# Keys and values of all eight batches formed at the head of each attention and kept; in the second attention GpSimd adds the mixture's sum to x, and VectorE's order is changed

## The reference

```python
x = x + L0_xcond(layernorm(x), ctx, ctx, tau, delta, ...)   # attention to 64 context rows, 16 heads of 16
x = x + L0_ffn(layernorm(x), ...)     # 8 experts, top 2; then layernorm(out + input) * ln_g + ln_b
x = x + L1_xcond(...)                 # the second attention
x = x + L1_ffn(...)
x = x + L2_xcond(...)                 # another kind of attention, with a window
x = x + L2_ffn(...)                   # 8 experts, top 2
x = x + L3_xcond(...)                 # the third attention
x = x + L3_ffn(...)

def xcond(q, k, v, tau, delta, ...):  # x is (8, 512, 256), k = v = ctx is (8, 64, 256)
    qh, kh, vh = q @ Wq.T + bq, k @ Wk.T + bk, v @ Wv.T + bv
    a = softmax((qh . kh * tau + delta) / 4)
    return (a . vh) @ Wo.T + bo
```

## Time and profile before

| | |
|---|---|
| median of 3 runs | 2288.46 us (2286.05 to 2291.26) |
| the profiled execution | 2285.1 us, its span 2283.3 us |
| busy | PE 86%, PEld 64%, DVE 57%, ACT 41%, POOL 26% |
| first attention | 8 us to about 215 us |
| second attention | 631 us to about 870 us |
| third attention | 1888 us to about 2100 us |

### The profile page before, as it was taken

The page is one execution under the profiler, slowest core; times in us unless marked ns, Lnnn a source line. Parts: engine busy times, 40 slices in busy tenths (PEclk is TensorE's granted clock), DMA queues, the critical chain, the costliest instruction groups (busy, mean ns, idle before and its releaser), DMA issues. The chain is left out here.

```text
span 2283.3 us, 37863 instructions
## 1 busy us (share of the span) xinstructions
PE 1963.4 (86%) x11930; PEld 1465.4 (64%) x11931; DVE 1310.2 (57%) x2973; ACT 941.4 (41%) x2050; POOL 593.6 (26%) x582
## 2 busy tenths in 40 slices
PE   6998569999848887999989739999999995998687
PEld 3665536666525553666666729999999983665355
DVE  5885456666558887787655162222222215887987
ACT  3444324444336543333222413333333323553787
POOL 1122246666424431011000032222222221321000
PEclk9999579999959998999989559999999997999899
DMA  7001211111141104000000611111111114100001
GB/s 268 1 1 56 77 49 63 61 64 60 53 162 56 56 1 162 0 1 0 0 15 5 240 33 33 37 34 37 34 37 37 37 31 157 40 20 1 10 28 38
DMA packets 71122, 119.54 MB, mean 52 GB/s; under 512 B 13648, under 2 KB 54736, under 8 KB 67952
## 3 DMA queue, kind: packets, MB, share of 16 engines
q1 hardware_dynamic: 55760, 78.76, 9.9%
q0 software_dynamic: 13680, 37.37, 5.2%
q10 hardware_dynamic: 1584, 2.13, 0.3%
HBM read 86.90 MB, written 31.33 MB: 52 GB/s over the span
## 5 line engine op out<-in xcount | busy, mean ns | idle before, releaser
L1421 ACT ACTIVATE e_hT<-psum,x_bt 128x128 f32<-128x128 f32 x568 | 154.6, 383 | 336.4 <-PE psum L1384 331.7
L1384 PEld LDWEIGHTS psum<-e_xT,e_w 128*128 128x128 f32 x2272 | 268.3, 194 | 8.4 <-ACT e_xT L1414 4.9
L268 POOL TENSOR_TENSOR rstd<-lnt,half 128x4 f32<-128x4 f32 (+1 forms) x72 | 73.3, 1018 | 769.6 <-DVE lnt L262 769.6
L1384 PE MATMUL psum<-e_xT,e_w 128*128 128x128 f32 x2272 | 268.9, 277 | 4.2 <-ACT e_xT L1414 4.2
L1393 PE MATMUL psum<-m_w,e_hT 128*128 x1136 | 256.8, 379 | 0.0
L1393 PEld LDWEIGHTS psum<-m_w,e_hT 128*128 128x128 f32 x1136 | 210.4, 190 | 25.7
L1442 DVE COPY e_w<-m_w 128x2048 f32 x71 | 87.1, 1227 | 234.4 <-PE psum L1384 230.0
L724 DVE TENSOR_REDUCE a_mx<-psum 128x8 f32<-128x512 f32 x192 | 123.2, 684 | 84.0 <-PE psum L515 83.4
L1241 ACT ACTIVATE e_hT<-psum,x_bt,x_gt 128x128 f32<-128x128 f32 x284 | 106.9, 457 | 142.1 <-PE psum L1208 142.1
L1325 POOL DMA_INDIRECT rows_out<-e_y,dst x106 | 106.0, 1000 | 205.7 <-DVE e_y L1452 175.0
L1317 POOL DMA_INDIRECT e_x<-rows_in,src x142 | 142.3, 1002 | 56.8 <-issue 35.2
(11 more groups left out here) (282 smaller groups left out, 3588.2 us busy)
## 6 DMA issues: line engine op xcount, KB each, us to landing
m_w<-in_L_ffn_w SPq DMA_DIRECT2D x16, 1024.0 KB, 9.3
m_w<-in_L_ffn_w SPq DMA_DIRECT2D x16, 512.0 KB, 12.7
rows_in<-r_work SPq DMA_DIRECT2D x16, 512.0 KB, 5.4
m_w<-rows_out SPq DMA_DIRECT2D x16, 512.0 KB, 5.9
a_ar_g<-rows_out SPq DMA_DIRECT2D x16, 512.0 KB, 5.0
x_res<-in_x SPq DMA_DIRECT2D x8, 512.0 KB, 7.1
m_w<-rows_in SPq DMA_DIRECT2D x8, 512.0 KB, 3.9
out_x<-x_res SPq DMA_DIRECT2D x8, 512.0 KB, 3.0
```

What stands on the lines that cost most here:

```text
L1384: mm = pe.matmul(h_b[s][:, f, :], w1[:, kk, f * P:(f + 1) * P], xT[s][:, kk, :], start=(kk == 0), stop=(kk == DC - 1))
L1421: g = act.activation(hT[s][:, f, :], h_b[s][:, f, :], ACT.Gelu, bias=bt[:, bass.ds(e * FC + f, 1)])
```

## The change

All three attentions: the tile `kv` (8 batches x 256 columns) holds keys and values without bias. PE forms them for batches 0 to 3 ahead of `turn(0)`, into the banks that scores and transposes use later, and those of batches 4 to 7 right behind them in the second and third attention, behind the first scores in the first. ACT copies two batches at a time to `kv`, ahead of everything else that it does (in the first attention the last two copies stand behind the queries). DVE's `drain_keys` and `drain_values` read `kv` and not PSUM, and `drain_keys(b + 1)` stands at t == 1 in place of `drain_keys(b + 2)` at t == 3. PE's `keys_values` at t == 3 is gone. SP issues the eight context loads ahead of x (first attention) or between the first and the second fetch (the others). Second attention: `add_sum(b + 2)` goes from DVE's t == 2 to GpSimd, behind `gain(b + 2)` and ahead of `sum(b + 3)`.

```diff
@@ sync
+                if coming:
+                    coming.fetch(sp, 0)
                 for b in range(NB):
-                    if loading and b:
+                    sp.dma_start(cx[:, b, :, :], a["ctxT"][b]).then_inc(cx_in[b], 16)
+                if coming:
+                    coming.fetch(sp, 1)
+                if loading:
+                    for b in range(1, NB):
                         load_x(sp, k, b)
-                    if coming and b < 2:
-                        coming.fetch(sp, b)
-                    sp.dma_start(cx[:, b, :, :], a["ctxT"][b]).then_inc(cx_in[b], 16)
@@ gpsimd
                             normed.gain(pool, b + 2)
+                            normed.add_sum(pool, b + 2)
                         if b + 3 < NB:
                             normed.sum(pool, b + 3)
@@ tensor
                     if c == 0:
                         pe.wait_ge(z_done, b + 1)
-                        pe.wait_ge(k_done, b + 1)
-                        pe.wait_ge(v_done, b + 1)
+                        wait_pos(pe, drained, DRAINS * b)
...
-                    wait_pos(pe, drained, DRAINS * b)
+                    kv_at = kv_b[b // 2][:, b % 2 * (2 * P):(b % 2 + 1) * (2 * P)]
...
-                    mm.then_inc(filled, 1)
+                    if b % 2:
+                        mm.then_inc(kv_ps, 1)
...
-                        if t == 3 and b + 2 < NB:
-                            keys_values(b + 2)
...
-                keys_values(0)
+                for b in range(NB // 2):
+                    keys_values(b)
+                if coming:
+                    for b in range(NB // 2, NB):
+                        keys_values(b)
...
+                pe.wait_ge(kv_in, NB // 4)
                 scores(0, 0, 0)
-                keys_values(1)
+                if not coming:
+                    for b in range(NB // 2, NB):
+                        keys_values(b)
+                pe.wait_ge(kv_in, NB // 2)
@@ scalar
+                def keep_keys_values(i):
+                    act.wait_ge(kv_ps, i + 1)
+                    act.activation(kv[:, 2 * i:2 * i + 2, :], kv_b[i].rearrange("p (b q) -> p b q", b=2),
+                                   ACT.Copy).then_inc(kv_in, 1)
+
+                for i in range(NB // 2 if coming else NB // 4):
+                    keep_keys_values(i)
                 if normed:
                     normed.normalise_sum(act, 0)
                 normalise(0)
@@ vector
-                            pr_b[:, None, c * S:(c + 1) * S].to_broadcast([P, HPG, S]), bk[:, c:c + 1],
+                            kv[:, b, None, c * S:(c + 1) * S].to_broadcast([P, HPG, S]), bk[:, c:c + 1],
...
-                            drain_keys(b + 2, s)
...
-                        if normed and t == 2 and b + 2 < NB:
-                            normed.add_sum(dve, b + 2)
+                        if t == 1 and more:
+                            drain_keys(b + 1, 1 - s)
```

More of the change, by code:

```diff
@@ L365, in attention @@
         cx = sb(nm + "cx", [P, NB, DC, S])
+        kv = sb(nm + "kv", [P, NB, 2 * P])
         z = sb(nm + "z", [P, TPB, D])
@@ L393, in attention @@
         split, d_in = sem(nm + "split"), sem(nm + "d_in")
+        kv_ps, kv_in = sem(nm + "kv_ps"), sem(nm + "kv_in")
+        kv_b = sc_b + [bank.rearrange("p i q -> p (i q)") for bank in tr_b]
         loading, k.loading = k.loading, False
@@ L405, in attention @@
             part = [sb(f"{nm}part{j}", [P, NB * S], BF16) for j in range(DSPLIT)]
-        FILLS, KV, ZT, Q = 5, 1, 2, 4
+        FILLS, ZT, Q = 4, 1, 3
         DRAINS = 4
@@ L492, in keys_values @@
                     pe.wait_ge(cx_in[b], 16)
-                    wait_pos(pe, drained, DRAINS * b)
+                    kv_at = kv_b[b // 2][:, b % 2 * (2 * P):(b % 2 + 1) * (2 * P)]
                     for c in range(DC):
                         for kk in range(DC):
-                            pe.matmul(pr_b[:, c * S:(c + 1) * S], w["k"][:, kk, c * P:(c + 1) * P],
+                            pe.matmul(kv_at[:, c * S:(c + 1) * S], w["k"][:, kk, c * P:(c + 1) * P],
                                       cx[:, b, kk, :], start=(kk == 0), stop=(kk == DC - 1))
@@ L499, in keys_values @@
                         for j in range(2):
-                            mm = pe.matmul(pr_b[j * S:(j + 1) * S, P:2 * P], cx[:, b, kk, :],
+                            mm = pe.matmul(kv_at[j * S:(j + 1) * S, P:2 * P], cx[:, b, kk, :],
                                            w["v"][:, kk, :].rearrange("p (c j e) -> p c j e", c=H // 2, j=2)[:, :, j, :],
                                            start=(kk == 0), stop=(kk == DC - 1))
-                    mm.then_inc(filled, 1)
+                    if b % 2:
+                        mm.then_inc(kv_ps, 1)
                 def scores(n, s, t):
@@ L676, in _ @@
                     drain_queries(0, 0, c)
+                if not coming:
+                    for i in range(NB // 4, NB // 2):
+                        keep_keys_values(i)
                 if normed:
@@ L698, in drain_keys @@
                 def drain_keys(b, s):
-                    dve.wait_ge(filled, FILLS * b + KV)
+                    dve.wait_ge(kv_in, b // 2 + 1)
                     for c in range(DC):
@@ L714, in drain_values @@
                             va[s][h, :, j, :],
-                            pr_b[h, P:2 * P].rearrange("p (c e) -> p c e", c=H // 2),
+                            kv[h, b, P:2 * P].rearrange("p (c e) -> p c e", c=H // 2),
                             bv[h, :].rearrange("p (c j e) -> p c j e", c=H // 2, j=2)[:, :, j, :], ALU.add)
@@ L828, in _ @@
                 softmax(0, 0)
-                drain_keys(1, 1)
                 for b in range(NB):
@@ L1550, in gain, with add_sum @@
         eng.tensor_tensor(u, u, self.g[:, None, :].to_broadcast([P, TPB, D]), ALU.mult).then_inc(self.u_scaled, 1)
-    def add_sum(self, dve, b):
+    def add_sum(self, eng, b):
         xs = self.k.x[:, b * (TPB * D):(b + 1) * (TPB * D)].rearrange("p (t d) -> p t d", t=TPB)
-        dve.wait_ge(self.u_scaled, b + 1)
-        dve.tensor_tensor(xs, xs, self.u[b % 2], ALU.add).then_inc(self.x_done, 1)
+        eng.wait_ge(self.u_scaled, b + 1)
+        eng.tensor_tensor(xs, xs, self.u[b % 2], ALU.add).then_inc(self.x_done, 1)
     def statistics(self, dve, b):
```

## The result

The changed kernel takes 2325.64 us (median of 4 runs, 2323.28 to 2327.05) against 2287.26 us (4 runs of the kernel before beside it, 2281.55 to 2291.26): a ratio of 1.0169, 95% interval 1.0149 to 1.0188. It is slower by about 38 us; forecast were 10. The profiled execution took 2324.3 us with a span of 2322.5, 39.2 more than that of before.

What follows compares the result with a forecast made beforehand. PE was taken to bound the first attention, a chain over several engines the second, the third between. -1.4 + 5.7 + 5.6 = +9.9 us on 2285.1, plus 3.4 for the median: 2298; range 2283 to 2311.

Steps and rivals of the forecast that it cites:

- The clock in the stream: Heads: eight batches of keys and values in a row, two at low clock and six at high, take 15.7 us.
- Second head, +10.9: Second attention's head: the norm of the sum starts 11.8 us later; +10.9 us, bounds +8 to +19.
- The slack of 0.9: Second attention's head: DVE took up the norm of the sum 0.9 us after its end; used up first.
- Third head, +6.6: Third attention's head: middle of +8.8 us and +4.3 us, the latter if the clock stays high.
- First attention, -1.4: First attention, whole: head 8.3 us longer, loop 9.7 us shorter (six batches, 1.62 each); -1.4 us.
- the middle (8.3): First attention's second scores: between +11.4 us and +5.2 us, the latter with the clock high throughout.
- Second loop, -5.2: Second attention's loop: with one GpSimd turn lost per batch by DVE, -5.2 us in all.
- the rival of two turns lost: Second attention's loop: DVE falls behind GpSimd twice a batch, +4.4 us for -5.2, so 2308; chance 0.19.
- the middle of three cases: Second attention's loop: no lost turn -14.8 us, one -5.2, two +4.4; the prediction took -5.2.
- Third loop, -1: Third attention's loop: 1 us gained for all six batches, bounds 0 and 9.7.
- the argument from ACT's wait: Third attention's loop: ACT waits 3.97 us for the next batch's shift; that chain bypasses keys and values, hiding their 1.62 us.
- I count nothing: Keys' drain at t == 1: GpSimd's bias addition can hold it, but DVE idles at that tile's end; 0 us.

Runs made afterwards that it cites:

- the kernel with the narrow keys apart: Changed kernel with second and third attention's keys all formed ahead of all values, by 64-column matmuls, against the same with 512-column matmuls; ratio 1.0165 to the kernel before.
- both repairs: Changed kernel with keys by 512-column matmuls in second and third attention, and GpSimd's sums split around the addition; ratio 1.0009 to the kernel before.

## Why the prediction was wrong

The sign was right, and so was the path through the heads, from PE's stream over ACT's last copy to the norm. Two steps were not: that PE at work would lift the clock within the stream, and that DVE would lose one turn at the port in a batch. The time lies 15 us above the range. Of the 29.3 us between the forecast of 9.9 and the measured 39.2, 12.7 are in the two heads, 10.9 in the second attention's loop and 3.6 in the third's.

- **The clock in the stream: the step that failed.** "I take two batches at the low clock and six at the high: 15.7." It was all eight at the low one, 23.60 us, just under the bound of 23.9 that the text itself gave. The reason given, that PE has nothing to wait for, so the clock should rise, was true in its first half. What shows the form of the keys to be the cause is the pair of kernels with keys of 512 and of 64 columns in the same order. The Trainium skill ("TensorE: Matmul & The Clock Gate", What's actually happening) says that "activity releases the throttle". By that the stream should have lifted the clock. The trace disagrees for the narrow keys, 23.60 us with PE busy throughout, and agrees for the wide ones, 0.61 in the mean of their 5.93 us and 1.00 behind. Why the form matters is not settled: the narrow keys have PEld as busy as PE and the wide ones have not, but the values have it too.
- **Second head, +10.9, measured +14.1.** The norm of the sum started 24.20 us after the first keys (forecast 16.6, before 4.81): +7.6. The slack of 0.9 was there (8.4 from norm to a_z, before 9.2). PE waited 11.06 us. From a_z to the scores it took 13.0 in place of 15.0, since the clock rose this time within the queries; and the first context, which landed sooner, gave 2.5.
- **Third head, +6.6, measured +16.1.** 7.6 by the same term, and 1.8 because the clock was still 0.54 from transposes to scores, where I had taken half of the gain of a clock that stays high.
- **First attention, -1.4, measured +0.3.** The loop gave 9.7 as forecast (t == 3 of 4.94). To the second scores it took 10.2 us more: above the middle (8.3), within the bounds (5.2 to 11.4). The stream ahead was at the low clock, the one behind at the high one. This is not the same each time: the kernel with the narrow keys apart has the same first attention, and in its profiled execution the second scores came 14.8 us behind the first and not 8.4.
- **Second loop, -5.2, measured +5.7: the second step that failed.** It lost two turns at the port in a batch, where the sum took one. This was the rival of two turns lost, which had 0.19; the turn is 29.28 where that rival said 29.7. The signs were named as L254, L258 or L262, on the idea that GpSimd gets in where DVE pauses for its own result. It got in between two instructions that DVE issued 0.08 us apart, as soon as its own work before had ended: L255 and L259. L259 has one SBUF input and was held just so. The Trainium skill ("SBUF — State Buffer", Who interferes with whom) lists tensor_scalar among the operations that can take the shared ports; the trace agrees, with 2.34 us for L259. I took the middle of three cases with no row for it.
- **Third loop, -1, measured +2.6.** The turn stayed at 24.01, so the argument from ACT's wait held. Two turns took 24.65 and 24.81, with the clock at 0.93 in the window, and the first one 1.2 longer. That PE idles more and the clock falls there fits, but no run took it apart.
- **Drains from SBUF.** "I count nothing" held. In the changed kernel a drain of keys in the loop took 1.25 us for its two instructions (0.88 in the head), and DVE idled behind it. In the one with both repairs it took 3.38, and the turn in which nothing else was lost was 0.1 us longer than with the keys left in PSUM.

The range was too narrow because the clock's two ends, for three heads at once, were treated as if they would average; they have one cause, and went the same way in both heads that matter. Eight batches at 0.50 in two heads alone are 15 us. The prediction's own bounds, all heads cold and two turns lost, add up to about 2330 (2298.4, 8.2 for each of two streams, 2.3 for the third attention's clock, 3.1 for the first attention and 9.6 for the loop); its range ended at 2311.

## What to carry to other kernels

Moving work off a bound engine's loop to its idle head pays only if the head does not wait for it: here it delayed a norm by 19 us in one stage and 16 in another, and saved nothing in their loops, which PE did not bound. Price PE's work in a cold stretch at the low clock unless a row shows that same form of matmul lifting it, and merge matmuls that share a weight: in the same order, that took 10 us off each of two heads. When an instruction goes to GpSimd, look at what else it then has ready: of a row without a pause, each instruction can hold up one of DVE's short ones for its whole length, twice a turn here. The same addition on GpSimd, with GpSimd's pause where DVE's chain stands, made the kernel 13 us faster than before; but by a margin of 0.10 us, so look at the rows again after any other change.

## What the hardware showed unexpectedly

- PE fully busy for 23.60 us at a granted clock of 0.50, and the same 128 instructions in 12.94 us at 1.00 behind wide matmuls.
- The same four batches at the same place in two kernels, at 1.00 in one profiled execution (6.56 us) and at 0.50 in the other (11.88).
- Values of eight batches in a row: 3.71 us at 1.00, 0.46 a batch, where alternating with narrow keys a row of eight shows 0.66.
- A DVE instruction on 128x4 elements of 0.16 us held for 2.32 to 2.38 us, twice in one chain of seven, by GpSimd's instructions that started 0.01 to 0.06 us ahead of it.
